# Cross-attention on one core: weighing two context tiles in one stretch, and filling the key stacks by SBUF-to-SBUF transfers

## What is computed

```
x = x + xattn(layernorm(x), ctx, ctx)        # x: 256 x 512, ctx: 25088 x 512, 16 heads of 32

q = (query @ Wq.T) * 32 ** -0.5              # per head
k = ctx @ Wk.T
v = ctx @ Wv.T
scores = sigmoid(q @ k.T)                    # no softmax: no maximum, no sum
o = scores @ v                               # summed over the 25088 context rows
return o @ Wo.T
```

## Time and profile before

| | us |
|---|---|
| median of 3 runs | 2120.92 |
| span of the profiled execution | 2119.5 |
| cross-attention's loop over 196 tiles | about 27 to 1876 |
| PE busy | 2096.5 |
| ACT busy | 1361.7 |
| DVE busy | 1190.9 |
| POOL busy | 1022.3 |

### The profile page before, as it was taken

The page is one execution under the profiler, slowest core; times in us unless marked ns, Lnnn a source line. Parts: engine busy times, 40 slices in busy tenths (PEclk is TensorE's granted clock), DMA queues, the critical chain, the costliest instruction groups (busy, mean ns, idle before and its releaser), DMA issues. The chain is left out here.

```text
span 2119.5 us, 42205 instructions
## 1 busy us (share of the span) xinstructions
PE 2096.5 (99%) x15810; PEld 1632.6 (77%) x15812; DVE 1190.9 (56%) x1495; ACT 1361.7 (64%) x1702; POOL 1022.3 (48%) x900
## 2 busy tenths in 40 slices
PE   9999999999999999999999999999999999988999
PEld 6777777777777777777777777777777777746998
DVE  6656556565565665656556565565655656525422
ACT  7666666666666666666666666666666666632764
POOL 5066564665646656466564665646656460000000
PEclk9999999999999999999999999999999999999999
DMA  5111211112111121111211112111121110122774
GB/s 179 42 60 40 74 45 61 58 40 74 45 61 57 40 74 45 62 57 40 74 45 63 56 40 74 45 63 56 40 74 45 63 56 21 65 101 112 277 278 168
DMA packets 43908, 157.09 MB, mean 74 GB/s; under 512 B 5600, under 2 KB 5600, under 8 KB 31200
## 3 DMA queue, kind: packets, MB, share of 16 engines
q1 hardware_dynamic: 43872, 156.59, 20.5%
HBM read 154.47 MB, written 0.52 MB: 73 GB/s over the span
## 5 line engine op out<-in xcount | busy, mean ns | idle before, releaser
L302 ACT ACTIVATE probs<-sc 128x1024 f32<-128x1024 f32 x784 | 761.6, 1022 | 371.5 <-PE sc L463 366.8
L352 DVE TENSOR_TENSOR k_stack<-kp,k_stack 32x512 fp32r<-32x512 f32 x772 | 529.5, 686 | 720.0 <-ACT k_stack L295 701.8
L295 ACT ACTIVATE k_stack<-kp 32x512 fp32r<-32x512 f32 x772 | 456.3, 591 | 257.4 <-PE kp L443 243.2
L267 POOL TENSOR_TENSOR piece_hi<-piece,zero 128x512 fp32r<-128x512 f32 x176 | 220.1, 1251 | 666.6 <-DMA piece<-w_all_dram 642.6
L463 PEld LDWEIGHTS sc<-rows_r,k_stack 96*128 96x128 f32 x3136 | 413.2, 190 | 100.0 <-issue 83.6
L463 PE MATMUL sc<-rows_r,k_stack 96*128 96x256 f32 x3136 | 460.1, 289 | 0.9 <-DMA k_stack<-k_stack 0.9
L454 PE MATMUL vp<-weights_r,c_hi 128*128 128x512 f32 x1568 | 392.9, 392 | 0.0
L443 PE MATMUL kp<-c_hi,weights_r 128*128 128x512 f32 x1544 | 386.8, 392 | 0.0
L474 PE MATMUL acc<-probs,v 128*32 128x256 f32 x6272 | 381.3, 382 | 0.1
L454 PEld LDWEIGHTS vp<-weights_r,c_hi 128*128 128x128 f32 x1568 | 282.0, 189 | 51.2 <-issue 0.8
L443 PEld LDWEIGHTS kp<-c_hi,weights_r 128*128 128x128 f32 x1544 | 277.2, 188 | 49.8
(11 more groups left out here) (135 smaller groups left out, 882.8 us busy)
## 6 DMA issues: line engine op xcount, KB each, us to landing
ctx_raw<-ctxT_dram SPq DMA_DIRECT2D x49, 1024.0 KB, 4.8
piece<-w_all_dram SPq DMA_DIRECT2D x178, 256.0 KB, 4.7
w_raw<-w_all_dram SPq DMA_DIRECT2D x44, 1024.0 KB, 4.8
weights<-wqk_dram SPq DMA_DIRECT2D x2, 1024.0 KB, 6.1
probs<-wqT_dram SPq DMA_DIRECT2D x1, 1024.0 KB, 6.0
probs<-wkT_dram SPq DMA_DIRECT2D x1, 1024.0 KB, 8.0
probs<-wvT_dram SPq DMA_DIRECT2D x1, 1024.0 KB, 11.9
k_stack<-k_stack SPq DMA_DIRECT2D x4, 256.0 KB, 3.0
```

The costliest lines, as they stand in the source:

```text
L267: nc.gpsimd.tensor_tensor(piece_hi[:], piece[:, t % 2, :], zero[:].to_broadcast([P, PIECE]), ALU.add).then_inc(piece_rounded, 1)
L295: nc.scalar.activation(kst[0:D, par, j, g, :], source[D * j:D * (j + 1), :], ACT.Copy).then_inc(k_hi, 1)
L302: nc.scalar.activation(probs[:, t % 2, g, :], sc[g % 2][:], ACT.Sigmoid).then_inc(probs_ready, 1)
L352: nc.vector.tensor_tensor(kst[D:2 * D, par, j, g, :], source[D * j:D * (j + 1), :], f32(kst[0:D, par, j, g, :]), ALU.subtract).then_inc(k_ ...
```

## The change

**Weighing.** PE does `v_project` for the tile in hand instead of the next one, and `weigh` runs only on odd tiles, for tiles t - 1 and t, one behind the other. `last_chunk` is gone; the last chunk runs the same code without `k_project`.

**Key stacks** (all chunks but the first, whose stack is made as before). ACT rounds `kp` once, 128 x 512, into a staging tile `kr_hi`; DVE subtracts once, 128 x 512, into `kr_lo`. SP copies from these into the stack: per tile 4 heads x 2 copies of hi and 4 x 1 of lo, 12 transfers of 32 rows of 2 KB (64 KB). `k_round` waits until the hi transfers of the tile before have landed, `k_difference` the same for lo, `k_project` waits for `k_split` (DVE's subtraction), and PE waits at each chunk's start until all hi and lo transfers have landed.

**SP's order.** Per tile the 12 transfers, then one piece; the context chunk's load comes at the chunk's end.

```diff
+        kr_hi, kr_lo = sb("k_rows_hi", [P, CH], F32R), sb("k_rows_lo", [P, CH], F32R)
...
+        K_HI_SENT, K_LO_SENT = 2 * HG * 16, HG * 16
...
             def one(c, par, first, k_next, split_next, load_next, looped):
-                if load_next:
-                    sp.wait_ge(ctx_split, c + 3)
-                    sp.dma_start(raw[:], ctxT[c + 3]).then_inc(ctx_loaded, 16)
-                if looped:
-
-                    for n in range(2, TC + 2):
+                for t in range(TC):
+                    if k_next:
+                        to = kst[:, 1 - par, :, t, :]
+                        sp.wait_ge(k_rounded, c * TC + (t + 1))
+                        for j in range(HG):
+                            rows = f32(kr_hi[D * j:D * (j + 1), :])
+                            sp.dma_start(f32(to[0:D, j, :]), rows).then_inc(k_hi_stacked, 16)
+                            sp.dma_start(f32(to[2 * D:3 * D, j, :]), rows).then_inc(k_hi_stacked, 16)
+                        sp.wait_ge(k_split, c * TC + (t + 1))
+                        for j in range(HG):
+                            sp.dma_start(f32(to[D:2 * D, j, :]), f32(kr_lo[D * j:D * (j + 1), :])
+                                         ).then_inc(k_lo_stacked, 16)
+                    if looped:
+
+                        n = t + 2
                         u = c - 1 if n < TC else c % UNITS
                         sp.wait_ge(piece_used, c * TC + (n - 2 - TC + 1))
...
+                if load_next:
+                    sp.wait_ge(ctx_split, c + 3)
+                    sp.dma_start(raw[:], ctxT[c + 3]).then_inc(ctx_loaded, 16)
...
+            def k_round(c, t):
+                act.wait_ge(k_made, c * TC + (t + TC + 1))
+                if not (isinstance(c, int) and c == 0 and t == 0):
+                    act.wait_ge(k_hi_stacked, c * (TC * K_HI_SENT) + t * K_HI_SENT)
+                nc.scalar.activation(kr_hi[:], kp[:], ACT.Copy).then_inc(k_rounded, 1)
...
                     if k_next:
-                        k_rows(tile + TC, 1 - par, t, kp[:])
+                        k_round(c, t)
...
+            def k_difference(c, t):
+                dve.wait_ge(k_rounded, c * TC + (t + 1))
+                if not (isinstance(c, int) and c == 0 and t == 0):
+                    dve.wait_ge(k_lo_stacked, c * (TC * K_LO_SENT) + t * K_LO_SENT)
+                nc.vector.tensor_tensor(kr_lo[:], kp[:], f32(kr_hi[:]), ALU.subtract).then_inc(k_split, 1)
...
                     if k_next:
-                        k_rest(tile + TC, 1 - par, t, kp[:])
-                    if k_next or t < TC - 1:
-                        v_out(tile + 1, (t + 1) % 2, not (first and t == 0))
+                        k_difference(c, t)
+                    v_out(c * TC + t, t % 2, not (first and t < 2))
+                if split_next:
+                    split_chunk(c + 2, par)
...
                 if not first:
-                    pe.wait_ge(k_lo, (c + 1) * G * HG)
-                    pe.wait_ge(k_dup, c * G)
-                if not k_next:
-                    return last_chunk(c * TC, par)
+                    pe.wait_ge(k_hi_stacked, c * (TC * K_HI_SENT))
+                    pe.wait_ge(k_lo_stacked, c * (TC * K_LO_SENT))
                 for t in range(TC):
                     tile = c * TC + t
+                    opening = first and t == 0
                     for g in (0, 1):
...
+                        scores(tile * G + g, par, t, g, not opening)
+                    if k_next:
+                        chunk_ready = ()
+                        if t == 0:
+                            chunk_ready = (((ctx_hi, c + 2),), (), ((ctx_split, c + 2),))
+                        if not opening:
+                            pe.wait_ge(k_split, tile)
+                        k_project(1 - par, t, kp[:], before=chunk_ready or ((), (), ()))
...
-                    ahead = t + 1 if t < TC - 1 else 0
-                    v_project(tile + 1, par if ahead else 1 - par, ahead, True)
-                    for g in range(G):
-                        weigh(tile, t, g)
+                    if opening:
+                        pe.wait_ge(wv_split, 1)
+                    v_project(tile, par, t, not opening)
+                    if t % 2:
+                        for done in (t - 1, t):
+                            for g in range(G):
+                                weigh(c * TC + done, done, g)
```

More of the change, by code:

```diff
@@ L155, in cross_attention @@
         ctx_hi, ctx_split = sem("ctx_hi"), sem("ctx_split")
-        k_made, k_hi, k_lo, k_dup = sem("k_made"), sem("k_hi"), sem("k_lo"), sem("k_dup")
+        k_made, k_hi, k_lo = sem("k_made"), sem("k_hi"), sem("k_lo")
+        k_rounded, k_split = sem("k_rounded"), sem("k_split")
+        k_hi_stacked, k_lo_stacked = sem("k_hi_stacked"), sem("k_lo_stacked")
         k_dup0 = [sem(f"k_dup_of_first{g}") for g in range(G)]
@@ L347, in split_chunk, with k_rest @@
                                         ALU.subtract).then_inc(ctx_split, 1)
-            def k_rest(u, par, g, source, copied=False):
+            def k_rest(u, par, g, source):
                 for j in range(HG):
@@ L353, in k_rest @@
                                             f32(kst[0:D, par, j, g, :]), ALU.subtract).then_inc(k_lo, 1)
-                if not copied:
-                    nc.vector.tensor_copy(kst[2 * D:3 * D, par, :, g, :],
-                                          kst[0:D, par, :, g, :]).then_inc(k_dup, 1)
+            def k_difference(c, t):
[3 more added lines that the diff above has]
+                nc.vector.tensor_tensor(kr_lo[:], kp[:], f32(kr_hi[:]), ALU.subtract).then_inc(k_split, 1)
             def v_out(m, buf, free):
@@ L373, in _ @@
             for g in range(G):
-                k_rest(g, 0, g, k_first[g], copied=True)
-            v_out(0, 0, False)
+                k_rest(g, 0, g, k_first[g])
             def one(c, par, first, k_next, split_next, load_next, looped):
                 for t in range(TC):
[L379 to L382, removed]
                     if k_next:
-                        k_rest(tile + TC, 1 - par, t, kp[:])
-                    if k_next or t < TC - 1:
-                        v_out(tile + 1, (t + 1) % 2, not (first and t == 0))
+                        k_difference(c, t)
+                    v_out(c * TC + t, t % 2, not (first and t < 2))
+                if split_next:
+                    split_chunk(c + 2, par)
             chunks(dve, one)
@@ L432, in _, with k_project @@
             last.then_inc(q_made, 1)
-            def k_project(u, par, g, to, free, before=((), (), ())):
-                if free:
-                    pe.wait_ge(k_lo, u * HG)
+            def k_project(par, g, to, before=((), (), ())):
                 n = 0
@@ L478, in weigh @@
                     last.then_inc(probs_used, 1)
-            k_project(0, 0, 0, k_first[0], False, before=(
+            k_project(0, 0, k_first[0], before=(
                 ((wk_hi_done, 1), (ctx_hi, 1)), ((wk_split, 1),), ((ctx_split, 1),)))
             for g in range(1, G):
-                k_project(g, 0, g, k_first[g], False)
+                k_project(0, g, k_first[g])
             pe.wait_ge(q_lo, HG)
@@ L498, in zero_sums @@
                                      skip_group_check=True)
[L500 to L513, removed]
@@ L523, in one @@
                     for g in (0, 1):
-                        if first and t == 0:
+                        if opening:
                             first_stack(g)
[L526 to L533, removed]
```

## The result

The changed kernel takes **2359.96 us** (median of 4 runs, 2353.9 to 2361.43) against 2120.57 (2119.6 to 2122.44): the ratio is 1.1125, 95% interval 1.111 to 1.1141. It is slower by 239 us. Slower was forecast, but by 52 us, and the range ended at 2250.

A forecast was written before the change was run, and what follows sets the result against it. The prediction took PE, busy 99% of the span, as the bound. From 2120.9 us, -31 for pairing and +1 at the ends gave 2091; +82 for waits at chunk starts gave 2173, range 2085 to 2250.

The forecast's parts named there:

- Part 1: PE weighs two tiles in one stretch, sparing one way in and out per pair: 96 pairs, -31 us.
- s: Time PE loses on one way into and out of weigh: 0.33 us, 3.5% of a tile.
- part 3: Last and first chunk: +5.6 us waiting for sigmoids, -4.6 for dropped switches, taken as +1 us.
- part 2: ACT's four activations (2.44 us) become one (0.60), DVE's subtractions one (0.69); gains no time itself.
- Part 4: SP's 12 transfers per tile, 0.55 us each, make PE wait 1.7 us at 48 chunk starts: +82 us.
- the prediction's own chain: From k_project through k_round and SP's issues: last lo lands at 12.85 us, PE wants the chunk at 11.08.
- The rival on the clock: The chunk-start wait lets TensorE's clock fall to half: another 82 us, 2255; chance within 0.08.
- B: Rival: SP issues the transfers at 0.33 us, no wait at chunk starts, 2091 us; chance 0.20.
- C: Rival: SP's issues near 0.43 us, wait 0.9 us per chunk, 2134 us; chance 0.05.
- A: The forecast case: SP's issues of 0.50 to 0.64 us, PE waits at each chunk start, 2150 to 2250; chance 0.62.

The follow-up runs named there:

- the fastest version: Kernel with weigh in pairs alone, but ACT rounds two heads into the stack, DVE two, and one 256 KB transfer makes the third rows: 2097.87 us, ratio 0.9898.
- the clock held: The changed kernel with 14 matmuls of zeros on PE ahead of the wait at each chunk start: 2253.59 us, ratio 1.0628.

## Why the prediction was wrong, by its own steps

**Part 1, the pairing: right.** Pairs without a wait take 18.60 us; 18.59 was worked out, from s = 0.33 (the two equations give 0.32 when they are solved, which changes nothing). The best version that keeps them is 22 us under the kernel before, of the 30 that parts 1 and 3 gave together.

**Parts 2 and 3: right as far as they go.** ACT and DVE are in time: PE waits for neither in the chunks that make keys. In the last chunk it waits for ACT as part 3 has it: in the fastest version a tile's scores take 3.35 us there (1838.52 to 1841.87 in its timeline), 1.3 more than 2.01, where 1.4 was taken. But part 2 priced the staging at no gain. The runs with pairs alone show that it, or something like it, is a condition of the pairing: without it ACT and DVE cost 95 us (2186 against the 2091 of parts 1 and 3). The prediction had asked only about the changed kernel, where this is in order.

**Part 4, the place: right; the size of an issue: wrong. This is the step that failed first.** PE waits at each chunk's start, once per chunk and in nearly all for the last lo transfer. The landing is 2.0 (2.1 taken). The mis-sized term is the issue: 0.50, and 0.55 from start to start, were taken from L205's undisturbed value, and in a burst it is 0.59 and 0.63. The evidence was at hand and was set aside: L205's first issue, close behind another transfer, was 0.635, and the one that ended a burst of five 0.60. All twelve here but the first stand behind another. The error counts in more than one tile, since SP then isn't free when the odd tile's k_round is done: 0.8 us of carry-over from the even tile and 0.7 in the burst itself (6.9 us from its start to the start of the last issue, where 6.15 was taken) give a wait of 3.3 in place of 1.8 (1.7 in the sum). With 0.63 in place of 0.55 the prediction's own chain gives a wait of 3.4 and 2254 us; with the clock held, 2253.6 was measured (that close by some chance, since the wait is 3.3). So the chain was right and its term was not.

**The rival on the clock: wrongly dismissed.** The sum puts the clock at nothing. The rival was given no more than a part of 0.08, with "dense work on both sides" against it. Two rows had been read, one of 3.76 us idle with a fall and one of 1.26 without, and nothing between; the wait of 3.3 lies near the first. It cost 106 us, more than the prediction's whole forecast of +52. The two errors are tied: a wait that is longer by 1.6 us costs that itself, and it brings the fall from some of the chunk starts to all of them.

**The sum as it should have been:** pairs and ends 2091, as the forecast had it; waits 48 x 3.3 = 158, together 2249, measured 2253.6 with the clock held, so some 4 us have no place; the clock 106, together 2360 from the measured 2253.6. Of the 187 us between forecast and measurement, 77 are thus the wait (48 x 1.6), 106 the clock and 4 unplaced. The direction came out right by the cause that was forecast, the wait at the chunk's start.

**Rivals B and C** needed an issue below 0.42 and one near 0.43 (by the prediction's own chain B decides below 0.41). The least of all 2304 issues is 0.507, so both are out. The Trainium skill, DMA: Bandwidth & Descriptors, section Why a DMA increments its semaphore by 16 and not by 1, has the 512 cycles that the prediction turned into 0.43 us, an estimate. The trace disagrees with it, and the trace decides. A's own range of issues, 0.50 to 0.64, left out the dearest of L208, 0.682, though all eight were called for it.

## What to carry to other kernels

Price small transfers by the queue's issue time in a burst, not by their bytes and not by the issue of one that stands alone, and lay the whole list of the issuing queue against the tile, the carry-over from the last one too. A wait of PE that comes once per outer turn can cost more than itself, by what it does to the clock, and matmuls of zeros ahead of the wait tell the two apart in one run. When work is regrouped on the bound engine, ask for each operand who brings it, since an order that looks idle (values made one tile ahead) may be what hides an eviction.

## What the runs showed of the hardware

- An issue of 32 rows within SBUF takes 0.51 us on SP when its queue was idle before, and as a rule 0.58 to 0.60 behind another (median 0.59), whether it moves 64 KB (the changed kernel) or 32 (the run with twice the issues). From ACT it is about the same: 2.53 us from the start of the first to the end of the fourth. The one of 4 x 32 rows, 256 KB, takes 0.59 (the fastest version).
- From issue to landing such a transfer takes 1.8 us with 32 KB, 2.0 with 64 and 3.0 with 256, medians of the pages; the two smaller kinds were issued 0.63 apart, so landings overlap.
- TensorE's clock fell to half at all 48 chunk starts of the changed kernel, most with an idle of 3.2 to 3.4 us, and at 11 of 42 with one of 1.60 to 1.70 us in equal surroundings. With the idle time filled with matmuls of zeros it stayed at full in a kernel that was otherwise the same.
